# Four banks for the hidden values, a routing end written out by hand, and a lag of four chunks in a mixture-of-experts kernel

## The reference, cut to what matters

```
h = layernorm(x) * (1 + ca) + sa
x = x + ga * attention(h)                    # causal linear attention, 64 wide, phi = elu + 1, then W_o
h = layernorm(x) * (1 + cb) + sb
logits = layernorm(h) @ router_w.T + router_b            # 8 experts
top_w, top_idx = top_k(logits, 2); top_w = softmax(top_w)
for e in range(8):
    t = layernorm(h, ln_g[e], ln_b[e])
    t = gelu(t @ w1[e] + b1[e]) @ w2[e] + b2[e]          # 256 -> 1024 -> 256
    out += combine[..., e] * t
x = x + gb * out
```

## Time and profile before

| | |
|---|---|
| median of 3 runs | 1141.53 us (1140.14 to 1142.62) |
| profiled execution | 1140.76 us, span 1139.0 us |
| instructions | 32684 |
| TensorE matmul / weight load busy | 991.4 us (87%) / 793.3 us (70%) |
| VectorE, ScalarE, GpSimd busy | 874.9 (77%), 629.8 (55%), 575.4 us (51%) |
| mean granted TensorE clock | 0.941 |
| moved by DMA | 118.92 MB |

### The profile page before, as it was taken

The page is one execution under the profiler, slowest core; times in us unless marked ns, Lnnn a source line. Parts: engine busy times, 40 slices in busy tenths (PEclk is TensorE's granted clock), DMA queues, the critical chain, the costliest instruction groups (busy, mean ns, idle before and its releaser), DMA issues.

```text
span 1139.0 us, 32684 instructions
## 1 busy us (share of the span) xinstructions
PE 991.4 (87%) x8083; PEld 793.3 (70%) x8084; DVE 874.9 (77%) x2878; ACT 629.8 (55%) x1356; POOL 575.4 (51%) x479
## 2 busy tenths in 40 slices
PE   5878889887467788888999999999999999999986
PEld 2545565555456666666888888888888888888864
DVE  7779998887867677667877778787777878777875
ACT  3668877765656656664454454545445454544553
POOL 3125766676575355553545454454545445454442
PEclk8889988888569999999999999999999999999999
DMA  5333544333875675754444454544434444444442
GB/s 173 90 90 122 165 153 131 131 113 116 217 217 144 121 166 107 170 86 95 62 79 72 68 84 76 93 75 83 74 66 77 74 82 72 77 82 77 79 76 36
DMA packets 172037, 118.92 MB, mean 104 GB/s; under 512 B 111900, under 2 KB 158664, under 8 KB 171960
## 3 DMA queue, kind: packets, MB, share of 16 engines
q0 software_dynamic: 32832, 54.88, 24.2%
q1 hardware_dynamic: 139128, 63.13, 23.5%
HBM read 78.01 MB, written 45.98 MB: 109 GB/s over the span
## 4 chain that ended last, share of the span: by engine, by line
PE 52%; DVE 7%; issue 6%; ACT 5%; SPq 1%; ACTq 0%; POOLq 0%; DVEq 0%; DMA 0%
PE banks L1533 26%; PE banks L1545 25%; DVE store L1184 2%; ACT xT L694 2%; ACT store L731 1%; ACT gf L702 1%; DVE xT L1379 1%; DVE store L1440 1%; DVE store L1438 1%; DVE rowbuf L1416 1%; DVE rowbuf L1426 1%; DVE nhl L1386 1%; ACT store L709 1%; SPq L431 0%; SPq L437 0%
## 5 line engine op out<-in xcount | busy, mean ns | idle before, releaser
L1533 PE MATMUL banks<-nhl,store 128*128 128x256 bf16 (+1 forms) x3408 | 454.6, 269 | 48.6 <-ACT gf L702 26.0
L1545 PE MATMUL banks<-store 128*128 (+1 forms) x3240 | 450.4, 274 | 8.6 <-DVE store L1440 8.0
L702 ACT ACTIVATE gf<-banks,b1t 128x256 f32<-128x256 f32 (+1 forms) x568 | 255.4, 460 | 353.7 <-PE banks L1533 341.0
L641 POOL DMA_INDIRECT out<-rowbuf,ydst x135 | 226.4, 1677 | 362.0 <-DVE rowbuf L1426 324.0
L1533 PEld LDWEIGHTS banks<-nhl,store 128*128 (+1 forms) x3408 | 318.5, 98 | 113.8 <-issue 64.4
L1545 PEld LDWEIGHTS banks<-store 128*128 128x128 bf16 x3240 | 307.9, 98 | 60.6 <-issue 13.7
L1440 DVE TENSOR_TENSOR store<-gf,store 128x256 bf16<-128x256 f32 (+1 forms) x568 | 233.8, 412 | 69.7 <-ACT store L709 52.7
L1438 DVE CAST store<-gf 128x256 bf16<-128x256 f32 (+1 forms) x492 | 146.9, 299 | 118.8 <-ACT gf L702 98.2
L599 POOL DMA_INDIRECT lists<-store,slot x128 | 137.5, 1074 | 80.0 <-DVE store L1117 45.8
L607 POOL DMA_INDIRECT csB<-y_rows,ygb x135 | 138.9, 1029 | 41.9 <-issue 41.9
L694 ACT ACTIVATE xT<-xT,gb 128x256 f32<-128x256 f32 (+1 forms) x142 | 76.0, 582 | 31.6 <-DVE xT L1379 29.7
(11 more groups left out here) (247 smaller groups left out, 1041.7 us busy)
## 6 DMA issues: line engine op xcount, KB each, us to landing
vk<-lists SPq DMA_DIRECT2D x256, 64.0 KB
b2t<-in_L_ffn_b SPq DMA_DIRECT2D x71, 128.0 KB
store<-in_L_attn_x SPq DMA_DIRECT2D x16, 512.0 KB, 5.2
out<-store SPq DMA_DIRECT2D x16, 512.0 KB, 3.2
store<-in_L_ffn_w SPq DMA_DIRECT2D x28, 256.0 KB
store<-in_L_ffn_w SPq DMA_DIRECT2D x7, 1024.0 KB, 8.5
csB<-mod_rows SPq DMA_DIRECT2D x16, 256.0 KB, 4.3
csB<-y_rows,ygb POOLq DMA_INDIRECT x135, 3.7
```

Of the source, the lines that this page charges most:

```text
L641: g.indirect_dma_start(out_rows, bass.IndirectOffsetOnAxis(ap=ydst[:, r, h:h + 1], axis=0), yt[:, r, h, :], None, compute_op=ALU.add).then ...
L702: a.activation(gf[:, c % 4, 0:halves(j) * P], hidden(j)[c % 2][:, 0:halves(j) * P], ACT.Gelu, bias=b1t[:, r, c:c + 1]).then_inc(gf_s, 1)
L1533: last = t.matmul(hidden(j)[c % 2][:, 0:halves(j) * P], w, nhl[:, r, m, 0:halves(j) * P], start=n == 0, stop=n == 5)
L1545: last = t.matmul(ACC[r][h][:, 0:D], g[:, c, h * P:(h + 1) * P], w, start=c == 0 and n == 0, stop=c == NI - 1 and n == 2)
```

## The change

Three things are done together.

1. Hidden values get four banks (`MM` is banks 0, 1, 6, 7), used by chunk number modulo 4, and `first` waits for the gelu of four chunks before. `LAG` is 4 in place of 3: `second` of chunk c follows `first` of chunk c + 4, the accumulators are read out at chunk 3 and gated at chunk 4.
2. The rows of the next tile are scaled in separate steps: half 0 after gelu 1, half 1 after gelu 2, rounding after gelu 3; `split_rows` is at chunk 5. Tile 0 prepares tile 1 in the same way. `SPLITS` begins with (2, 2, 1, 1, 2, 2, ...) and covers expert 1 too.
3. `pipeline` ends with step 15. What steps 16 to 20 did is written out on each engine in an order by hand, below. `early_tiles` is cut in eight parts between VectorE's work on the last block. Ranking of the last block on TensorE is at chunk 1 of tile 0, its slots on VectorE at chunk 0 of that tile, and TensorE waits at chunk 3 of tile 0 for the last logits, all four weight pieces and the last count. In the kernel before it waits for the four weight pieces ahead of tile 0 and for the other two ahead of tile 1.

SP's order of DMAs is unchanged.

```diff
-LAG = 3
+LAG = 4
+        LOG_END = V[:, 0:NC * E]
-        MM = bank[6:8]
-        MM0 = bank[4:6]
+        MM = (bank[0], bank[1], bank[6], bank[7])
-            for i in range(NB + 5):
+            for i in range(NB):
-        SPLITS = (1, 1, 1, 1, 1, 2, 2, 2, 2, 2, 2, 2, 2, 1, 2)
+        SPLITS = (2, 2, 1, 1, 2, 2, 2, 2, 2, 2, 2, 2, 2, 2, 2)
-            return 2 + k // 4, k % 4 // 2, k % 2
+            return 1 + k // 4, k % 4 // 2, k % 2
@@ gpsimd, after pipeline(g, step)
+            g.tensor_tensor(wog[0:H, 1, 0:D], wo[:, :], gaB[:, 1, :], ALU.mult).then_inc(wog_s, 1)
+            placed(NB - 5, (0,))
+            inverse_root(NB + 1, 1)
+            placed(NB - 5, (1, 2, 3))
+            inverse_root(NB + 2, 0)
+            inverse_root(NB + 3, 1)
+            placed(NB - 4, range(NC))
+            placed(NB - 3, range(NC))
+            pool.wait_ge(gb_out, 16)
+            pool.wait_ge(h2_s, NB)
+            gb_rows(0, 0)
+            placed(NB - 2, range(NC))
+            gb_rows(1, 1)
+            placed(NB - 1, range(NC))
@@ scalar, gelu(j, half, r)
-                    if c == 1 and not (isinstance(j, int) and (j == 0 or j + 1 >= TILES)):
-                        head_rows(j + 1, half + r, 1 - r)
+                    if not (isinstance(j, int) and j + 1 >= TILES):
+                        if c in (1, 2):
+                            scale_rows(j + 1, 1 - r, c - 1)
+                        if c == 3:
+                            head_rows(j + 1, 1 - r)
@@ scalar, after pipeline(a, step)
+            a.activation(ktok[:, 1, :, :].rearrange("p c h -> p (c h)"), V[:, 0:NC * H], ACT.Copy).then_inc(ktok_s, 1)
+            normed(NB - 3)
+            differences(NB - 5)
...
+            routed(NB - 4)
...
+            turned(NB - 4)
+            normed(NB - 2)
+            routed(NB - 3)
+            turned(NB - 3)
+            normed(NB - 1)
+            differences(NB - 4)
+            routed(NB - 2)
+            for n in range(2):
+                head_of(0, 0, n)
+            turned(NB - 2)
+            head_of(0, 1, 0)
+            routed(NB - 1)
+            differences(NB - 3)
+            head_of(0, 1, 1)
+            turned(NB - 1)
+            differences(NB - 2)
+            for k in range(NK):
+                scale_rows(0, 0, k)
+            head_rows(0, 0)
+            differences(NB - 1)
@@ vector, tile
+                    if c == 0 and first:
+                        placed(NB - 1)
-                    if c == 0 and not first and not last_tile:
+                    if c == 0 and not last_tile:
                         turn(j + 1, half + r, 1 - r)
-                    if c == 3 and not first and not last_tile:
+                    if c == 5 and not last_tile:
                         split_rows(j + 1, half + r, 1 - r)
@@ vector, after pipeline(v, step)
+            stats(rows(NB - 2), 1)
+            placed(NB - 5)
...
+            modulated(NB - 3)
+            moments(NB + 2, stats_before(NB + 1))
...
+            neg_mean_rstd(NB + 1, 1)
+            dve.wait_ge(rden_s, NB)
+            for c in range(NC):
+                last = v.scalar_tensor_tensor(rows(NB - 1)(c), SO[c][:, 0:D],
+                                              rden[:, c:c + 1], rows(NB - 1)(c), ALU.mult, ALU.add)
+                if c + 1 == NC:
+                    last.then_inc(x2_s, 1)
+                early_part(c)
...
+            for c in range(NC):
+                last = v.bn_stats(st[:, 1, c, :], rows(NB - 1)(c))
+                if c + 1 == NC:
+                    last.then_inc(st_s, 1)
+                early_part(NC + c)
+            logits(NB - 4)
+            modulated(NB - 2)
+            moments(NB + 3, stats_before(NB + 2))
+            absent_ranks()
+            neg_mean_rstd(NB + 2, 0)
+            highest(NB - 4)
+            choose(NB - 4, 0)
+            logits(NB - 3)
+            dve.wait_ge(nm_s, NB + 4)
+            modulated(NB - 1)
+            moments(NB + 4, stats_before(NB + 3))
+            placed(NB - 4)
+            neg_mean_rstd(NB + 3, 1)
+            highest(NB - 3)
+            choose(NB - 3, 1)
+            logits(NB - 2)
+            highest(NB - 2)
+            placed(NB - 3)
+            choose(NB - 2, 0)
+            turn(0, 0, 0)
+            picked(NB - 2)
+            for n in range(2):
+                rest_of(0, 0, n)
+            split_rows(0, 0, 0)
+            logits(NB - 1)
+            highest(NB - 1)
+            choose(NB - 1, 1)
+            doubled(NB - 2)
...
+            destinations(0, 0, 0)
+            for n in range(2):
+                rest_of(0, 1, n)
@@ tensor
-                wait_past(pe, gf_s, NI * j + c - 1)
+                wait_past(pe, gf_s, NI * j + c - 3)
-                        last = t.matmul(hidden(j)[c % 2][:, 0:halves(j) * P], w, nhl[:, r, m, 0:halves(j) * P], start=n == 0, stop=n == 5)
+                        last = t.matmul(MM[c % 4][:, 0:halves(j) * P], w, nhl[:, r, m, 0:halves(j) * P], start=n == 0, stop=n == 5)
@@ tensor, after pipeline(t, step)
...
+            last.then_inc(score_s, 1)
+            ranked(NB - 5)
...
+            last.then_inc(pv_s, 1)
+            turned(NB - 4)
...
+            last.then_inc(owo_s, 1)
+            logits(NB - 4)
+            absent_ranks()
+            turned(NB - 3)
+            logits(NB - 3)
+            ranked(NB - 4)
+            turned(NB - 2)
+            logits(NB - 2)
+            ranked(NB - 3)
+            turned(NB - 1)
+            ranked(NB - 2)
+            logits(NB - 1)
             first_early_waits()
             for c in range(NI):
+                if c == 1:
+                    ranked(NB - 1)
+                if c == 3:
+                    pe.wait_ge(lg_s, NB)
+                    pe.wait_ge(rest_s, 4)
+                    pe.wait_ge(base_s, NB)
+                    hold(pe, "pe")
                 tile_chunk(0, 0, 0, True, own, own, c)
```

More of the change, by code:

```diff
@@ L815, in step @@
                     last.then_inc(nT_s, 1)
[L816 to L825, removed]
                 if attend:
@@ L1687, in _, with turned, logits @@
             pipeline(t, step)
+            def turned(b):
+                pe.wait_ge(nrm_s, b + 1)
+                pe.wait_ge(hT_s, NB)
+                pe.wait_ge(nT_s, b)
+                for k in range(NK):
+                    for c in range(NC):
+                        last = t.transpose(TR[k][:, c * P:(c + 1) * P], nrm[:, b % NR, c, k * P:(k + 1) * P], ident[:, :])
+                last.then_inc(nTp_s, 1)
+            def logits(b):
+                pe.wait_ge(ktok_s, NB)
+                pe.wait_ge(lg_s, b)
+                pe.wait_ge(nT_s, b + 1)
+                for c in range(NC):
+                    for k in range(NK):
+                        last = t.matmul(LOG_END[:, c * E:(c + 1) * E], nT[:, k, c * P:(c + 1) * P], rTg[:, k, :], start=k == 0, stop=k == NK - 1)
+                last.then_inc(log_s, 1)
@@ new lines, in ranked @@
+            def ranked(b):
+                pe.wait_ge(ohs_s, b + 1)
+                pe.wait_ge(x2_s, min(b + 4, NB))
+                flat = ohs[:, :, :].rearrange("p c e -> p (c e)")
+                pe.wait_ge(base_s, b)
+                hold(pe, "pe")
+                t.matmul(RANK.rearrange("p (c e) -> p c e", c=NC), onesf[0:1, 0:P], base[0:1, :].unsqueeze(1).to_broadcast([1, NC, E]), start=True, stop=False)
+                t.matmul(RANK, before[:, :], flat, start=False, stop=False)
+                for back in range(1, NC):
+                    t.matmul(O[:, back * E:NC * E], allone[:, :], flat[:, 0:(NC - back) * E], start=False, stop=back == NC - 1)
+                for c in range(NC):
+                    last = t.matmul(TOT, allone[:, :], flat[:, c * E:(c + 1) * E], start=c == 0, stop=c == NC - 1)
+                last.then_inc(rank_s, 1)
@@ new lines, in _ @@
+            pe.wait_ge(phi_s, NB)
+            pe.wait_ge(vT_s, NB)
+            pe.wait_ge(x2_s, NB - 1)
+            pe.wait_ge(lg_s, NB - 4)
+            pe.wait_ge(q2_s, NB)
+            for s in range(NC):
+                at = slice(0, H) if s % 2 == 0 else slice(H, 2 * H)
+                q_of = qk if s % 2 == 0 else q2
+                last = t.matmul(SC[s], vT[at, 1, s // 2 * P:(s // 2 + 1) * P], q_of[at, 1, s * P:T], start=True, stop=True)
+            last.then_inc(score_s, 1)
+            ranked(NB - 5)
@@ new lines, in _ @@
+            last.then_inc(pv_s, 1)
+            turned(NB - 4)
+            pe.wait_ge(strip_s, NB)
+            pe.wait_ge(qz_s, NB)
+            pe.wait_ge(oT_s, NB)
+            pe.wait_ge(wog_s, NB)
+            for c in range(NC):
+                last = t.matmul(SO[c][:, 0:D + 1], oz[:, 1, c * P:(c + 1) * P], wog[:, 1, :], start=True, stop=True)
+            last.then_inc(owo_s, 1)
[3 more added lines that the diff above has]
+            logits(NB - 3)
```

200 lines of the change are left out of this document (136 added, 64 removed).

## The result

The changed kernel takes 1100.45 us (median of 4, 1099.51 to 1103.39), the kernel before 1141.84 (4 runs): ratio 0.9644, 95% interval 0.9622 to 0.9665. The forecast was 1121.5: the sign right, the gain twice what I gave it, and outside the range. The profiled execution took 1100.65 (span 1098.9).

A forecast was written before the change was run, and what follows sets the result against it. VectorE's chain was to pace the early tiles, with TensorE already 96% busy in the loop. Gains 8.3 - 0.5 + 7.0 + 5 = 19.8 off a median of 1141.53 gave some 1121.5, range 1107 to 1133.

The forecast's parts named there:

- Loop, "I take 0": 24 loop passes: TensorE 96% busy, nothing waits for a bank or rounded value, so gain 0.
- The sign that I had given for being right, passes of 22.1: Loop: passes of 22.1 would show the forecast right; passes above 22.3 would show it wrong, split_rows late.
- 0.8 of cover is left; if it went, each of 48 tiles would pay what it lacks.: Loop: split_rows ends 5.7 after chunk 3's start, next tile starts at 6.55; taken as no loss.
- The drain: Routing's end before tile 0: chain through four engines, first expert matmul at 315.7, 13.9 earlier; tile 1 at 333.0.
- Early tiles: Tiles 5 to 14: VectorE's chain to split_rows paces a tile at 12.2, not 13.19; gain 7.0 in sum.
- tile 7: Tile 7 gets worse: ScalarE's bias wait becomes 4.4 and the tile 16.6, bounds 14.5 and 19.
- Tile 5: Tile 5 still carries the end of VectorE's table work, 1.5, so it takes 13.7.
- tiles 1 to 4: Tiles taking over expert 1's weight pieces: 14.7, 13.5, 14.6 and 14.4, together 57.2 against 56.7, loss 0.5.
- The rival of the clock: Half clock through tiles 0 and 1 gives 1134 (0.08); through tiles 0 to 4 about 1158, slower than before (0.05).
- Half tiles: Half tiles at the end: ten TensorE waits for gelu, sum 4.6, and small followers go; gain 5 (3 to 6).

The follow-up runs named there:

- late condition: Same programs unedited, TensorE's semaphore updates reaching other engines late: kernel before 1151 to 1154; changed kernel 1184.80 beside 1152.90, ratio 1.0261.
- normal condition: Same programs unedited, without the late semaphore updates: changed kernel 1100.45, kernel before 1141.84, ratio 0.9644.

## Why the prediction was wrong in size

- **Loop, "I take 0". The step that failed** is the first one: "Nothing waits there for a bank or a rounded value, so the change has nothing to take". I read "issue" as a fixed cost of the edge, with no engine to blame. It was TensorE's queue, 2.1 for branch and load behind its wait for VectorE's low part of chunk 4, which the earlier trace rows do not name. At 23 edges 0.93 to 1.06 goes each, 22.2 in all; small steps (groups 1.36 to 1.42 apart in place of 1.31) were 0.2 a pass, 4.5; and at loop entry the first groups no longer run at the 1.2 GHz level (up to 1.28 from one group to the next in place of 0.66, behind the wait of 2.02), 1.7. These three are the 28.4. The sign that I had given for being right, passes of 22.1, did not come: they are 20.96.
- **"0.8 of cover is left; if it went, each of 48 tiles would pay what it lacks."** The mechanism was right and I gave it no chance of its own. In the late condition the cover goes, most tiles pay 0.7, and the loop takes 36.9 more than in the normal one (540.0 against 503.1); with 16 more up to tile 1 and 29 more in the tiles 1 to 14 the kernel is slower than before.
- **The drain: right.** Scaling of block 14 at 289.75 (forecast 289.2), variance 294.40 (294.0), block 15's scaling 299.12 (298.6), variance 303.78 (303.5), first expert matmul 315.74 (315.7), tile 1 at 332.61 (333.0). Two steps of my sum are off in small: 281.1 and 1.82 make 282.9, not 283.05, and with 5.9 the scaling comes at 288.9, not 289.2. In the late condition nothing of it is left: first matmul at 332 to 337 beside 330 to 336.
- **Early tiles: pace right.** 12.27 forecast as 12.2, behind split_rows as said (1.62). Term mis-sized: tile 7 took 17.9, not 16.6 (its bias wait 6.3, not 4.4). Tile 5 took 14.7, not 13.7: after the wait of 3.6 for split_rows at its start its groups run 2.5 apart in place of 1.3 for 5 us, at the 1.2 GHz level. The 2.4 lost on tiles 1 to 4 can be the clock's in part at most: tile 1 took 16.1 (forecast 14.7) at a granted clock of 0.89, tile 2 14.8 (13.5) at 1.00, and tile 3, at 0.88, was shorter than forecast (14.2 against 14.6); what made tile 2 longer stays open. The rival of the clock was right in kind, not in size: it was at the 1.2 GHz level for up to 5 us behind the waits at the starts of tiles 1, 3 and 5 (2.3, 3.0, 3.6), not behind tile 2's (3.5), and never for a whole tile. The Trainium skill ("TensorE: Matmul & The Clock Gate", section "A second HAM failure mode: psum-queue depth-cycling") tells of a clock that swings in a kernel which cycles through banks and idles briefly between groups. Here the loop rotates through four banks with no idle time between groups and shows 1.00 over 503 us: rotation alone does not lower the clock, and the page's own case, rotation with idle time all along, no run here shows.
- **Half tiles: mis-sized.** 1.7, not 5. The waits for gelu fell from 4.6 to 1.0 as said, but waits for split_rows of 3.2 came in their place.

## What to carry to other kernels

Idle time put down to "issue" at a loop's edge is not free of causes: look at the branch and register loads of that engine's queue, and at the last wait that it had to pass before them; anything that ends that wait earlier (lag, or the order on the other engine) buys the edge back. When work that the next tile needs is moved later, weigh the cover that is left against the lateness that a signal can have, not against zero: here one chunk of 1.3 us took the loop from 540.0 to 505.8 in the late condition and cost nothing in the normal one. Weigh pairs of such moves too: split_rows at chunk 5 is harmless there with lag three (passes of 21.08 and 21.24), lag four is harmless with split_rows at chunk 3 (21.34), and only both together lose. The version to keep has split_rows at chunk 4 and tile 7's loads first (0.967 where the changed kernel has 1.030; in the normal condition only the first of its two edits was measured, 0.963).

## What the hardware showed

In the late condition TensorE's semaphore updates reach the others late, by 1.4 at gelu 3 of most loop tiles (no gelu of the loop starts more than 0.12 late in the normal one). The strongest case is in the end of the routing: DVE's timeline, then PE's, with the matmuls that it waits for.

```profile
308.43 0.37 DVE L1130 MAX8 mx<-lg 128x8 f32<-128x8 f32 x4
314.59 0.22 DVE L1182 TENSOR_TENSOR pick<-oh,banks 128x64 f32<-128x64 f32 x1 [5.79 <-remote]
```
```profile
308.69 0.25 PE L1881 MATMUL banks<-ohs,allone 128*128 128x8 bf16 x4
```

The ranks are done at 308.94 and used at 314.59; in the normal condition 308.76 and 308.94. Besides these matmuls that instruction waits for nothing but VectorE's own earlier work, long done.

Late updates are not all of it. In tile 1 of the same run TensorE itself stands still inside a group, between single matmuls, with no engine named (timeline of PE):

```profile
354.60 0.38 PE L1697 MATMUL banks<-nhl,store 128*128 128x256 bf16 x2 [0.61 <-issue]
356.01 0.27 PE L1697 MATMUL banks<-nhl,store 128*128 128x256 bf16 x1 [1.04 <-issue]
357.44 0.37 PE L1697 MATMUL banks<-nhl,store 128*128 128x256 bf16 x1 [1.16 <-issue]
359.57 0.37 PE L1697 MATMUL banks<-nhl,store 128*128 128x256 bf16 x1 [1.75 <-issue]
```

Tile 1 takes 21 to 27 in every run of the late condition, with either end of the routing, and 13 to 16 in the normal one. Such stops inside a group stand in some of the late runs and in none of the normal ones.

The records of the late runs are thinner as well. From 100 us on they lack about 15 to 22% of the engines' semaphore updates, the normal runs less than 2%, and they hold 7400 to 9000 updates from landing DMAs, the normal runs 14400 to 14700, for the same transfers. Whether the recording holds the engines up, or both have one cause, stays open: every time here comes from a recorded execution. That the landing of DMAs is what holds the updates up is argued from the coincidence in time, not shown; nor is it known what puts a run into one condition or the other.
